# One subtraction per unit instead of two in a two-layer graph network kernel

## The chip, the cores and the metric

The kernel runs on one core of one Trainium2 chip. The metric is the device time of one execution in microseconds; lower is better.

## The reference

Two graph layers follow each other on 4096 nodes with 256 channels. The adjacency matrix `adj` is 4096 x 4096 in float32, 64 MB.

```python
def layer0(x, adj, w):
    A = adj + eye(4096)
    d = rsqrt(sum(A, axis=1))
    return elu(((A * d[:, None] * d[None, :]) @ x) @ w)
def layer1(x, adj, W, b):
    return relu((adj @ x) @ W.T + b)
x = layernorm(x + layer0(x, adj, w))
x = layernorm(x + layer1(x, adj, W, b))
```

## The kernel before

**Units and chunks.** The matrix is cut into chunks of 512 rows by 1024 columns (`raw`, 2 MB, four transfers of 512 KB issued on SP's queue) and each chunk into up to two units of 512 x 512. A unit is the amount that TensorE multiplies at one go. There are 128 units, and the text numbers them 0 to 127 in the order of the list `units`, in which every engine takes them. Units 0 to 28 belong to pass A (the row sums are made, and what of layer 0 can be multiplied already is), 29 to 91 to pass B (the rest of layer 0 and the first part of layer 1), 92 to 127 to pass C (the rest of layer 1). A "row" is a group of 512 nodes; eight of them are finished in B and eight in C. All 84 chunks are read from HBM again in each pass that needs them. `raw` has three buffers in A, and two from the first chunks of B on.

**What a unit goes through.** VectorE (DVE) turns it by a blockwise transposition (`turn`, L479, `turned`). ScalarE (ACT) rounds it to the short float format that TensorE takes (`hi`, L343, `a_hi`), in two halves of 128 x 1024. DVE subtracts, which gives the rest (`lo`, L496, `a_lo`), in two halves too. TensorE (PE) runs 24 matmuls of 128 x 512 on it (`product`, L710 to L712), half 0 first, then half 1: v_hi times a_hi, v_hi times a_lo, v_lo times a_hi. `turned`, `a_hi` and `a_lo` have two buffers each, taken in turns, so that unit u+2 writes where unit u was.

**The waits.** All go by counting semaphores; `halves_of(u, half)` is 2u + half + 1. PE asks for half 0 of `hi` and `lo` before its first twelve matmuls of a unit and for half 1 before the other twelve, and adds one to `s_used` after each half. `hi(u)` asks, half by half, that PE has used that half of unit u-2 and that `lo` of it is done. `turn(u)` asks for both second halves of u-2. An SP load of a chunk into a buffer asks that the last unit of the chunk before it in that buffer has been turned.

**The order on each engine** is written out by the loops over the chunks. On DVE it is turn(u), lo(u-1), turn(u+1), lo(u) and so on, in A as turn, turn, lo, row sums, lo where a chunk has two units. Between them come the steps of rows that are finished, each so many units after the row's last unit: `aggregate` (L545, two instructions, PSUM), `residual` (L556, or L561 and L565 in layer 1), and `v_low` (L525), which waits for `v_hi` from ACT. On ACT it is hi(u), and behind it the steps of a finished row: `elu_parts` (L395 to L401), `moments` (L410, L416), `normalise` (L428) with `v_hi` (L432) or the stores (L435). PE's own steps between units are `project` (L678), `project_x` (L657) and `fold_degrees` (L636).

The functions that the change touches, and what calls them:

Of the kernel before, what the change touches and what calls it, by code (L numbers as in the profile page):

```python
# [33 lines left out]
F32 = mybir.dt.float32  # L34
F32R = mybir.dt.float32r
ALU = mybir.AluOpType
# [4 lines left out]
def gnn_two_layers(nc: bass.Bass, x: bass.AP, adj: bass.AP, w: bass.AP, W: bass.AP, b: bass.AP, out: bass.AP):  # L41
# [96 lines left out]
    def halves_of(u, half):  # L138

        return 2 * u + half + 1  # L140


    HALVES = [(0, slice(0, GT // 2)), (1, slice(GT // 2, GT))]

    with ExitStack() as ctx:  # L145
        def sb(name, shape, dt=F32):
            return ctx.enter_context(nc.sbuf_tensor(name, shape, dt))

        def sem(name):
            return ctx.enter_context(nc.semaphore(name))  # L150
# [5 lines left out]
        turned = [sb(f"turned{i}", [P, GT, GN]) for i in range(2)]  # L156
        a_hi = [sb(f"a_hi{i}", [P, GT, GN], F32R) for i in range(2)]
        a_lo = [sb(f"a_lo{i}", [P, GT, GN], F32R) for i in range(2)]
# [49 lines left out]
        s_hi = sem("hi_halves_ready")  # L208
        s_lo = sem("lo_halves_ready")
        s_used = sem("halves_used")  # L210
# [258 lines left out]
        def _(dve):  # L469
# [19 lines left out]
            def lo(u):  # L489

                dve.wait_ge(s_turn, u + 1)
                for half, part in HALVES:
                    dve.wait_ge(s_hi, halves_of(u, half))
                    if u >= 2:
                        dve.wait_ge(s_used, halves_of(u - 2, half))
                    nc.vector.tensor_tensor(a_lo[u % 2][:, part, :], turned[u % 2][:, part, :],  # L496
                                            a_hi[u % 2][:, part, :].bitcast(F32),
                                            ALU.subtract).then_inc(s_lo, 1)

            def deg_part(n):  # L500
                _, row, panel, _ = chunks[n]
# [66 lines left out]
            def low_and_later(u):  # L568

                if lows_done[0] > u:  # L570
                    return
                lows_done[0] = u + 1
                lo(u)
                for a in ended(u, AGG_AT, rows_done):
                    aggregate(a)
                for a in ended(u, RESIDUAL_AT, rows_done):
                    residual(a)
                for a in ended(u, NORM_AT, rows_done):
                    if accs[a][2] == 0:
                        v_low(GROUPS + order_of[a], accs[a][1])  # L580
# [9 lines left out]
            for n, (name, row, panel, mine) in enumerate(chunks):  # L590
# [18 lines left out]
                if 0 <= last < DIAGONALS and at == 0:  # L609
                    deg_row(last)  # L610
            lo(U - 1)
            for u in range(U - 1, U + NORM_AT + 1):
                for a in ended(u, AGG_AT, rows_done):
# [142 lines left out]
```

## Time and profile before

| what | us |
|---|---|
| median of 3 runs | 953.71 |
| lowest and highest run | 950.77, 953.84 |
| span of the profiled execution, first to last instruction | 945.9 |
| PE busy, share of the span | 798.6, 84% |
| DVE busy | 736.0, 78% |
| ACT busy | 530.9, 56% |
| POOL busy | 101.9, 11% |

The profile is of one execution. It gives its span, and no time of its own beside that; the median of the runs is 7.8 us above the span, which is what lies before the first and behind the last instruction. In the views every row of a timeline begins with start and duration in microseconds from the start of the span; a row marked x2 holds two instructions back to back, and its duration runs from the start of the first to the end of the second. Brackets at its end give the idle time before it and what ended it.

### The profile page before, as it was taken

The page shows a single profiled execution, that of the slowest core. Times are in us where ns is not written, and L with a number is a line of the kernel's source. Part 1 is how long each engine was busy: PE and PEld are TensorE (multiplying, and loading weights), DVE is VectorE, ACT ScalarE, POOL GpSimd, SP SyncE. Part 2 cuts the span into 40 slices and gives each one's busy share as a digit, 9 for nine tenths or more (in the row PEclk, how much of TensorE's full clock was granted, in tenths as well). Part 3 has the DMA queues.
Part 4 walks back from the last instruction along what each step waited for, and adds up shares of the span by engine and source line. Part 5 has one row for each costly group of instructions (what it writes and reads, how often), then busy time and mean ns, then how long its engine had stood idle before and what let it go on. Part 6 is the DMA issues. An engine that isn't in the chain of part 4 may idle for free. (4 is left out here: it accounts for less than half of the span.)

```text
span 945.9 us, 10551 instructions
## 1 busy us (share of the span) xinstructions
PE 798.6 (84%) x3524; PEld 656.8 (69%) x3524; DVE 736.0 (78%) x537; ACT 530.9 (56%) x1192; POOL 101.9 (11%) x108
## 2 busy tenths in 40 slices
PE   0151756569989999999999999999999999999993
PEld 0041635457768888888888888888887778888882
DVE  0454636579979878989898898988987979888861
ACT  2153535367777764475676757667573665455352
POOL 0000000000000000021110211202110231122020
PEclk9995777788999999999999999999999999999997
DMA  9999999999999999998999999999999799998900
GB/s 215 221 219 221 221 220 220 221 225 238 228 230 227 203 206 216 208 219 180 199 209 197 201 207 193 212 191 220 195 211 212 171 211 209 219 219 181 198 23 22
DMA packets 191972, 190.08 MB, mean 201 GB/s; under 512 B 6960, under 2 KB 191920, under 8 KB 191920
## 3 DMA queue, kind: packets, MB, share of 16 engines
q1 hardware_dynamic: 187312, 185.23, 96.2%
q10 hardware_dynamic: 4608, 4.20, 1.5%
q8 instruction: 28, 0.46, 0.2%
q14 instruction: 24, 0.20, 0.1%
HBM read 185.20 MB, written 4.19 MB: 200 GB/s over the span
## 5 line engine op out<-in xcount | busy, mean ns | idle before, releaser
L710 PE MATMUL acc<-a_hi,v_hi 128*128 128x512 f32 x1024 | 411.7, 402 | 35.6 <-DVE a_lo L496 31.4
L343 ACT ACTIVATE a_hi<-turned 128x1024 fp32r<-128x1024 f32 x256 | 265.2, 1058 | 309.5 <-DVE turned L479 151.6
L711 PE MATMUL acc<-a_lo,v_hi 128*128 128x512 f32 x1024 | 406.3, 397 | 0.0
L712 PE MATMUL acc<-a_hi,v_lo 128*128 128x512 f32 x1024 | 406.0, 396 | 0.0
L479 DVE STREAM_TRANSPOSE turned<-raw 128x2048 f32<-128x2048 f32 x128 | 294.1, 2305 | 85.2 <-DMA raw<-in_adj_dram 78.6
L496 DVE TENSOR_TENSOR a_lo<-turned,a_hi 128x1024 fp32r<-128x1024 f32 x256 | 301.4, 1215 | 23.4 <-ACT a_hi L343 15.0
L710 PEld LDWEIGHTS acc<-a_hi,v_hi 128*128 128x128 f32 x1024 | 197.3, 193 | 80.3 <-issue 28.7
L712 PEld LDWEIGHTS acc<-a_hi,v_lo 128*128 128x128 f32 x1024 | 196.9, 192 | 42.3
L711 PEld LDWEIGHTS acc<-a_lo,v_hi 128*128 128x128 f32 x1024 | 197.4, 193 | 40.7
L353 ACT ACTIVATE acc<-raw 128x256 f32<-128x256 f32 x236 | 86.8, 368 | 47.1 <-DMA raw<-in_adj_dram 47.1
L503 DVE TENSOR_REDUCE deg_parts<-raw 128x10 f32<-128x2560 f32 (+4 forms) x32 | 78.1, 2444 | 27.0 <-DMA raw<-in_adj_dram 27.0
L636 PE MATMUL acc<-deg_sums,fold 128*32 128x4 f32 x64 | 2.1, 194 | 52.5 <-DVE deg_sums L512 52.5
L302 POOL TENSOR_TENSOR dinv<-deg,minus_half 128x4 f32<-128x4 f32 x8 | 11.0, 1375 | 329.2 <-DVE deg L520 329.2
L312 POOL TENSOR_TENSOR raw<-raw,x_row 128x1024 f32<-128x1024 f32 x8 | 22.1, 2763 | 223.3 <-ACT raw L399 223.3
L353 ACT ACTIVATION_READ_ACCUMULATOR acc<-raw 128x1 f32 x236 | 44.2, 187 | 0.0
L636 PEld LDWEIGHTS acc<-deg_sums,fold 128*32 128x32 f32 x64 | 1.4, 124 | 55.2 <-DVE deg_sums L512 54.5
L416 ACT ACTIVATE raw<-raw,minus_mean 128x256 f32<-128x256 f32 x64 | 31.8, 498 | 12.7 <-issue 6.4
L428 ACT ACTIVATE normed<-raw,shift,rstd 128x256 f32<-128x256 f32 x64 | 33.2, 590 | 8.1 <-POOL shift L332 8.1
L525 DVE TENSOR_TENSOR v_lo<-normed,v_hi 128x1024 fp32r<-128x1024 f32 x16 | 19.5, 1222 | 22.1 <-ACT v_hi L432 17.5
L410 ACT ACTIVATE raw<-raw 128x256 f32<-128x256 f32 x64 | 25.6, 402 | 19.0 <-DVE raw L565 19.0
L323 POOL TENSOR_SCALAR minus_mean<-sums 128x4 f32<-128x4 f32 x16 | 9.9, 621 | 239.4 <-ACT raw L410 239.4
L657 PE MATMUL proj<-w_sb,x_row 128*128 128x256 f32 x128 | 31.0, 398 | 1.1 <-ACT x_row L372 1.1
(43 smaller groups left out, 347.3 us busy)
## 6 DMA issues: line engine op xcount, KB each, us to landing
raw<-in_adj_dram SPq DMA_DIRECT2D x336, 512.0 KB, 10.4
x_row<-in_x_dram SPq DMA_DIRECT2D x64, 128.0 KB, 9.3
out_dram<-normed ACTq DMA_DIRECT2D x32, 128.0 KB, 2.7
w_sb<-in_L_gnn_w_dram SPq DMA_DIRECT2D x1, 256.0 KB, 12.4
normed<-in_L_gnn_W_dram SPq DMA_DIRECT2D x1, 256.0 KB, 10.7
b_sb<-in_L_gnn_b_dram SPq DMA_DIRECT2D x1, 128.0 KB, 10.1
```

The costliest lines, as they stand in the source:

```text
L343: nc.scalar.activation(a_hi[u % 2][:, part, :], turned[u % 2][:, part, :], ACT.Copy).then_inc(s_hi, 1)
L353: nc.scalar.activation(junk[:, i % JUNK, :], raw[buffer_of[n]][:, k, :], ACT.Copy, accum_out=deg_parts[:, row % 2, panel, k:k + 1]).then_i ...
L410: nc.scalar.activation(neg[:, t, :], res[:, t, :], ACT.Copy, accum_out=sums[:, t:t + 1]).then_inc(s_sums, 1)
L416: nc.scalar.activation(neg[:, t, :], res[:, t, :], ACT.Square, bias=minus_mean[:, t:t + 1], accum_out=squares[:, t:t + 1]).then_inc(s_sq, 1)
L428: nc.scalar.activation(normed[:, t, :], res[:, t, :], ACT.Identity, scale=rstd[:, t:t + 1], bias=shift[:, t:t + 1]).then_inc(s_norm, 1)
L479: ins = nc.vector.transpose(dst, src)
L496: nc.vector.tensor_tensor(a_lo[u % 2][:, part, :], turned[u % 2][:, part, :], a_hi[u % 2][:, part, :].bitcast(F32), ALU.subtract).then_inc ...
L503: nc.vector.tensor_reduce(deg_parts[:, row % 2, panel, mine], raw[buffer_of[n]][:, mine, :], AX_X, ALU.add).then_inc(s_degd, 1)
L657: ins = pe.matmul(proj[:, t, :], flat[:, GN * h + P * t:GN * h + P * (t + 1)], w_sb[:, h, :], start=(h == 0), stop=(h == CH - 1))
L710: pe.matmul(dst, v_hi[:, k, ch], a_hi[u % 2][:, t, :], start=begin, stop=False)
L711: pe.matmul(dst, v_hi[:, k, ch], a_lo[u % 2][:, t, :], start=False, stop=False)
L712: ins = pe.matmul(dst, v_lo[:, k, ch], a_hi[u % 2][:, t, :], start=False, stop=end)
```

## The change

`lo` becomes one subtraction over the whole unit, 128 x 2048. It waits for the second half of `hi(u)` and, from unit 2 on, for the second half of unit u-2 to have been used by PE, and then adds 2 to `s_lo` when it ends. Nothing else is edited: `hi` stays in halves, PE still asks half by half, and what others wait for on `s_lo` has the same numbers.

```diff
             def lo(u):
 
                 dve.wait_ge(s_turn, u + 1)
-                for half, part in HALVES:
-                    dve.wait_ge(s_hi, halves_of(u, half))
-                    if u >= 2:
-                        dve.wait_ge(s_used, halves_of(u - 2, half))
-                    nc.vector.tensor_tensor(a_lo[u % 2][:, part, :], turned[u % 2][:, part, :],
-                                            a_hi[u % 2][:, part, :].bitcast(F32),
-                                            ALU.subtract).then_inc(s_lo, 1)
+                dve.wait_ge(s_hi, halves_of(u, 1))
+                if u >= 2:
+                    dve.wait_ge(s_used, halves_of(u - 2, 1))
+                nc.vector.tensor_tensor(a_lo[u % 2][:], turned[u % 2][:], a_hi[u % 2][:].bitcast(F32),
+                                        ALU.subtract).then_inc(s_lo, 2)
```

## Rows read from the trace of the kernel before

**Rows 1.** Windows: length, busy per engine, granted clock, DMA share, GB/s.

```profile
0.00:280.00 280.00, 152.52 (x630) 122.32 (x631) 162.19 (x106) 136.97 (x437) 11.02 (x24) 0.86 1.12 223
280.00:926.00 646.00, 642.28 (x2880) 531.55 (x2878) 570.06 (x428) 388.04 (x736) 89.20 (x80) 1.00 0.95 197
```

**Rows 2.** DVE groups kept apart by shape: busy us, mean ns, idle before.

```profile
L496 DVE TENSOR_TENSOR a_lo<-turned,a_hi 128x1024 fp32r<-128x1024 f32 x256 | 301.4, 1215 | 23.4 <-ACT a_hi L343 15.0 <-issue 4.1 <-PE acc L712 3.5
L479 DVE STREAM_TRANSPOSE turned<-raw 128x2048 f32<-128x2048 f32 x128 | 294.1, 2305 | 85.2 <-DMA raw<-in_adj_dram 78.6 <-DVE a_lo L496 0.5
...
L486 DVE TENSOR_TENSOR turned<-turned,ident 128x128 f32<-128x128 f32 x32 | 7.2, 287 | 0.3
```

**Rows 3.** Timeline of DVE, 501 to 512 us.

```profile
501.31 1.23 DVE L525 TENSOR_TENSOR v_lo<-normed,v_hi 128x1024 fp32r<-128x1024 f32 x1 [2.17 <-ACT v_hi L432]
502.45 2.31 DVE L479 STREAM_TRANSPOSE turned<-raw 128x2048 f32<-128x2048 f32 x1
504.69 2.31 DVE L496 TENSOR_TENSOR a_lo<-turned,a_hi 128x1024 fp32r<-128x1024 f32 x2
509.34 2.32 DVE L496 TENSOR_TENSOR a_lo<-turned,a_hi 128x1024 fp32r<-128x1024 f32 x2
```

**Rows 4.** Timeline of PE: first matmuls of units 57 and 58.

```profile
506.21 0.39 PE L710 MATMUL acc<-a_hi,v_hi 128*128 128x512 f32 x1
...
511.65 0.39 PE L710 MATMUL acc<-a_hi,v_hi 128*128 128x512 f32 x1
```

**Rows 5.** Timelines of DVE and PE at unit 71.

```profile
583.22 2.32 DVE L496 TENSOR_TENSOR a_lo<-turned,a_hi 128x1024 fp32r<-128x1024 f32 x2
...
584.55 0.47 PE L710 MATMUL acc<-a_hi,v_hi 128*128 128x512 f32 x1 [0.20 <-DVE a_lo L496]
```

**Rows 6.** Timeline of ACT and DVE, from PE's wait to v_lo.

```profile
529.09 1.06 ACT L343 ACTIVATE a_hi<-turned 128x1024 fp32r<-128x1024 f32 x1 [1.61 <-PE acc L712]
...
534.26 2.00 ACT L343 ACTIVATE a_hi<-turned 128x1024 fp32r<-128x1024 f32 x2
...
539.00 1.06 ACT L432 ACTIVATE v_hi<-normed 128x1024 fp32r<-128x1024 f32 x1
...
540.09 1.23 DVE L525 TENSOR_TENSOR v_lo<-normed,v_hi 128x1024 fp32r<-128x1024 f32 x1 [2.16 <-ACT v_hi L432]
```

**Rows 7.** Timelines of DVE and PE at unit 18.

```profile
278.25 2.32 DVE L496 TENSOR_TENSOR a_lo<-turned,a_hi 128x1024 fp32r<-128x1024 f32 x2
...
279.58 0.47 PE L710 MATMUL acc<-a_hi,v_hi 128*128 128x512 f32 x1 [4.07 <-DVE a_lo L496]
```

**Rows 8.** Timelines of DVE and PE at units 43 and 85.

```profile
426.77 2.31 DVE L496 TENSOR_TENSOR a_lo<-turned,a_hi 128x1024 fp32r<-128x1024 f32 x2
...
428.22 0.40 PE L710 MATMUL acc<-a_hi,v_hi 128*128 128x512 f32 x1
...
660.92 2.32 DVE L496 TENSOR_TENSOR a_lo<-turned,a_hi 128x1024 fp32r<-128x1024 f32 x2
...
662.66 0.39 PE L710 MATMUL acc<-a_hi,v_hi 128*128 128x512 f32 x1
```

**Rows 9.** Timelines of DVE, ACT and PE around units 99 and 103.

```profile
742.65 3.73 DVE L496 TENSOR_TENSOR a_lo<-turned,a_hi 128x1024 fp32r<-128x1024 f32 x2
743.83 1.06 ACT L343 ACTIVATE a_hi<-turned 128x1024 fp32r<-128x1024 f32 x1 [1.61 <-PE acc L712]
...
774.67 2.32 DVE L496 TENSOR_TENSOR a_lo<-turned,a_hi 128x1024 fp32r<-128x1024 f32 x2
...
776.00 0.47 PE L710 MATMUL acc<-a_hi,v_hi 128*128 128x512 f32 x1 [1.20 <-DVE a_lo L496]
```

**Rows 10.** Timelines of ACT, DVE and PE at unit 127.

```profile
916.83 2.01 ACT L343 ACTIVATE a_hi<-turned 128x1024 fp32r<-128x1024 f32 x2 [1.94 <-issue]
...
917.98 2.36 DVE L496 TENSOR_TENSOR a_lo<-turned,a_hi 128x1024 fp32r<-128x1024 f32 x2 [4.13 <-issue]
...
920.51 0.39 PE L710 MATMUL acc<-a_hi,v_hi 128*128 128x512 f32 x1
```

## The prediction

> **What bounds the kernel now.** I read the windows first. From 280 to 926 us PE is busy for 642.3 of 646 us at the full granted clock; before 280 us it is busy for 152.5 of 280 us, while the DMA share stands at 1.12 and the adjacency comes in at 223 GB/s [rows 1]. So there are two stages: up to unit 18 the loads set the pace, and from there to the last unit PE does. The reader is to see that DVE, at 570 of 646 us, and DMA, at 0.95, are close behind PE in the second stage, but that neither is what ends last. A microsecond taken from DVE there is worth nothing by itself; a microsecond in which PE waits is lost, unless PE would have waited for something else later.
>
> The groups by shape give the prices on DVE: a subtraction of 1024 columns 1215 ns, of 128 columns 287 ns, a transposition of 2048 columns 2305 ns [rows 2]. The timelines then show how far ahead of PE the low halves are. This is the view that decides. PE starts unit 57 at 506.21 us and unit 58 at 511.65 us, 5.44 us apart [rows 4]. The two subtractions of unit 57 begin at 504.69 us and the pair ends at 507.00 us [rows 3]. PE starts while the second of them is still running: it needs only half 0 then, and asks for half 1 twelve matmuls (2.72 us) later.
>
> **The change part by part.** (1) *The instruction.* The pair takes 2.31 to 2.32 us from its first start to its last end [rows 3]. The two sizes of subtraction give (1215 - 287) / 896 = 1.036 ns a column and a fixed part of 287 - 128 x 1.036 = 154 ns [rows 2]. Two instructions already overlap (2 x 1.215 = 2.43 against 2.31 us), so of the 154 ns about 120 are hidden now. The trace shows no subtraction of 2048 columns. Below, it can cost 2.31 - 0.15 = 2.16 us; above, 2.31 us, which is what the transposition of the same width takes. I take 2.24 us, the middle, so 0.07 us less work on DVE per unit, 128 x 0.07 = 9 us in all. I cost this at nothing, since DVE is not what ends last in either stage.
>
> The Trainium skill (VectorE: DVE Perf Modes, Rules for kernel authors) says to minimise the count of DVE operations and not the semaphores, because the pipe is drained after each one anyway. That speaks for the change; with DVE as the bound the sum would be a gain of 9 us, and by the windows, where PE is the bound, it is none.
>
> (2) *The signal.* PE's wait for half 0 of `lo` now ends when the whole unit is done. Where PE waits for it in the trace, its first matmul starts 0.11 us after the first half ended: at unit 71 the pair starts at 583.22, its first half ends about 1.22 later, at 584.44, and PE starts at 584.55 us [rows 5]. The new start of PE can be no earlier than start of the subtraction + 2.24 + 0.11, that is + 2.35 us. At unit 57 this is 504.69 + 2.35 = 507.04 against 506.21 us: PE waits 0.83 us [rows 3, 4].
>
> I made this sum for all 128 units. In pass B the shortage comes back once per finished row, at the first low halves behind `v_low`. DVE stands 2.2 us there, waiting for `v_hi`, then takes 1.15 us for `v_low` and 2.24 us for the transposition in hand, and only then subtracts [rows 3]. Seven units have it: 0.90 at unit 43, 0.65 at 50, 0.83 at 57, 0.60 at 64, 1.02 at 71, 0.84 at 78, 0.61 at 85; the first and the last are 426.77 + 2.35 - 428.22 and 660.92 + 2.35 - 662.66 [rows 8]. Sum 5.45 us. After each, DVE's lead grows again (a turn and a pair are 4.65 us apart, from 504.69 to 509.34 [rows 3], against PE's 5.44), and the units between are in time once PE is shifted.
>
> Does each stall shift all that follows, or does DVE get back on time? The next `v_low` hangs on PE: `hi` waits for PE at 529.09, `moments` follow it on ACT without a gap to 534.26, then `hi` and `normalise`, `v_hi` ends at 540.06 and `v_low` starts at 540.09 us [rows 6]. Whatever PE loses, this chain passes on to DVE, so the next shortage is as large as before, and the stalls add up.
>
> At unit 18, where PE-bound running begins, the shortage is 278.25 + 2.35 - 279.58 = 1.02 us [rows 7]. PE has no gap after it that it could make this up in. It covers units 29 and 33, which would be short by 0.55 and 0.85 us by themselves, but whose subtractions are paced by loads and so not shifted. Units 2, 4, 7 and 9 are short by 1.02 too; there PE idles later anyway, and I cost them at nothing.
>
> (3) *The wait for both halves of hi.* In pass C `hi` follows the stores on ACT and is itself the late one. At unit 127 the two halves of `hi` run from 916.83 to 918.84, and the subtraction starts at 917.98, after the first [rows 10]. Now it starts at about 918.89 and PE at 918.89 + 2.35 = 921.24 against 920.51 us: 0.73 us. The same pattern at units 114 and 120 gives 0.71 and 0.78. Together 2.2 us. At unit 99 the pair takes 3.73 us because its second half waits for `hi`, whose second half ends at 744.89 [rows 9]; the merged one ends at 744.94 + 2.24 = 747.18 instead of 746.38, so the two turns behind it, the buffer of `raw` and SP's load into it (next in SP's queue) come 0.80 us later, and unit 103's transposition waits for that load. There the shortage itself is 774.67 + 2.35 - 776.00 = 1.02 [rows 9], less 0.07 for the one merged pair ahead of it. Units 92 and 95 are short by 0.91 and 1.02, but PE waits for loads in between, and I count them at nothing. With 0.2 us taken off for the merged pairs ahead of unit 97 this stretch gives 0.80 + 0.95 - 0.2 = 1.5 us.
>
> (4) The wait for `s_used` of half 1 of unit u-2 costs nothing: in B and C PE has begun unit u-1, or `hi` of half 1, which waits for the same, is the later one.
>
> **Sum.** 1.0 + 5.45 + 1.5 + 2.2 = 10.2 us. The span goes from 945.9 to 956.1 us, and the 7.8 us outside it stay: 953.71 + 10.2 = 963.9 us. 0.3% (2.9 us) is about what a measurement of this kernel can tell from no change.
>
> **The rivals.** *The merge pays (faster).* If DVE set the pace, 9 us would be won: 944.7 us. For it: DVE is idle only once per row in B, 2.2 us [rows 3], and once that idle time belongs to the loop the saved time counts. Against it: PE is busy 99.4% of the stage [rows 1], and `v_low` waits for a chain that begins at PE. It decides only if the merged instruction is so short that unit 57's end comes before PE: 506.21 - 0.11 - 504.69 = 1.41 us, under what any row allows. The page named above would have this as the case to expect. Chance 0.04.
>
> *The stalls do not add up.* A stall gives ACT and DVE time, and if `v_low` did not move with PE, every second shortage would be covered by the shift of the first. Then about half is left, 5 us: 958.8 us. For it: units 29 and 33 behave so. Against it: rows 6. Chance 0.16.
>
> *No change.* PE's queue absorbs it, for instance if the 0.23 us between matmuls could shrink after a wait. Nothing in the rows shows PE catching up. 953.7 us, chance 0.06.
>
> *More than the sum.* Shortages that I counted as covered (29 and 33: 1.4 us; 92 and 95: 1.9 us) come on top, and the merged instruction takes 2.31 us (12 stalls x 0.07 = 0.8): 968.0 us. Chance 0.16. A drop of PE's granted clock after a stall would lie there too; against it, the clock is 1.00 over the whole stage from 280 us, which has an idle time of 1.20 us in it already [rows 1, 9].
>
> **The numbers.** The forecast as summed has 0.58. Its own range is 961 to 967 us: 2.16 us instead of 2.24 takes 1.0 off, the stretch of units 92 to 103 may be 0.95 or less, and one covered stall more or less is 1 us. The range for 8 in 10 reaches to the case of half the stalls below and to the case above: 957 to 969 us. Faster 0.04; same, within 0.3%, 0.08 (the case of no change and a little of the half case); slower 0.88.
>
> **What would show it.** Rows of L496 x128 with a mean near 2.3 us (as a record, some 0.03 above the start-to-end price). PE's idle time put down to `a_lo` L496 in the stage from 280 us on grows from about 2 us in three places to about 12 us in some fourteen, each of 0.6 to 1.1 us, one per row of B, right behind `v_low`. DVE's busy time falls by 7 to 11 us. The period of a row in B, 38.8 us now (501.31 to 540.09 [rows 3, 6]), grows by 0.6 to 1.0 us. The granted clock stays 1.00. It would be wrong if the places are fewer (something else on ACT or DVE moved ahead), if the loads in C begin to be the later ones, or if the merged instruction costs more than 2.31 us.

## The result, and the profile after

The changed kernel takes 983.92 us (median of 4 runs, 978.01 to 985.05) against 953.05 us before (4 runs): ratio 1.0331, 95% interval 1.0292 to 1.0369, 31 us slower. The direction was as forecast; the size is three times the 10.2 us of the sum, and outside the range.

The head of the page after, with the groups that answer to [rows 2] (the subtraction is now L495, PE's matmuls L708 to L710):

```profile
span 981.8 us, 10423 instructions
## 1 busy us (share of the span) xinstructions
PE 806.4 (82%) x3524; PEld 658.7 (67%) x3524; DVE 739.1 (75%) x409; ACT 529.3 (54%) x1192; POOL 99.7 (10%) x108
...
L708 PE MATMUL acc<-a_hi,v_hi 128*128 128x512 f32 x1024 | 415.2, 405 | 64.3 <-DVE a_lo L495 60.3
L343 ACT ACTIVATE a_hi<-turned 128x1024 fp32r<-128x1024 f32 x256 | 265.0, 1057 | 338.8 <-PE acc L710 189.3
...
L495 DVE TENSOR_TENSOR a_lo<-turned,a_hi 128x2048 fp32r<-128x2048 f32 x128 | 300.4, 2347 | 65.7 <-ACT a_hi L343 64.6
...
L323 POOL TENSOR_SCALAR minus_mean<-sums 128x4 f32<-128x4 f32 x16 | 21.4, 1338 | 264.9 <-ACT raw L410 264.9
```

Half of the subtractions are gone, and DVE is busy for 739 us where it was 736. The prediction had it fall by 7 to 11 us; six subtractions of pass C that take 2.7 to 4.1 us bring about 9 us back. The idle time of DVE before the subtraction, waiting for `a_hi`, rose from 15.0 [rows 2] to 64.6 us. One row was not looked at in the prediction: GpSimd's `minus_mean`, 128 x 4 elements, now takes 1338 ns on average, while `var_eps`, of the same size and engine, takes 0.19 us.

The tile's own view gives the durations of the subtraction (min/median/max, in ns) and who waits for it, from 280 us on:

```profile
L495 DVE TENSOR_TENSOR a_lo<-turned,a_hi x110: 2244/2291/4134, 282.9 to 952.5; 128x2048 fp32r<-128x2048 f32 x110
...
  PE acc L708: 28.7, 18
```

The shortest is 2.244 us, the price that the prediction took; the median is 2.29 us, and four take 4.13 us. PE waits for the low halves 18 times. One of these waits is unit 18's, 7.4 us against 4.07 us before [rows 7]. The other 17 come to 21.3 us, up to 2.8 us each in pass C, where the prediction had about 12 us in some fourteen places.

**A first check of the yardstick.** The profiled execution of the changed kernel took 983.62 us with a span of 981.8, so 1.8 us lie around a span, and not the 7.8 us that stand ahead of the prediction. The first profile of the kernel before was of a quick execution. The two traces therefore differ by 35.9 us, of which some 4 us are not the change's. What is shifted where is read from the start of PE's first matmul of each unit. Against the first trace of before, the changed kernel's is later by 8.0 us at unit 29, 19.1 at unit 92, 19.2 at unit 107, and 35.9 at unit 127. Pass B loses 11 us and pass C 17 us, nearly all of it behind unit 107, in four steps at units 108, 113, 119 and 126.

**One step of pass C, unit 108.** Timelines of DVE, POOL and ACT (ACT's accumulator reads left out):

```profile
817.97 2.25 DVE L495 TENSOR_TENSOR a_lo<-turned,a_hi 128x2048 fp32r<-128x2048 f32 x1
820.36 2.31 DVE L479 STREAM_TRANSPOSE turned<-raw 128x2048 f32<-128x2048 f32 x1
824.58 4.13 DVE L495 TENSOR_TENSOR a_lo<-turned,a_hi 128x2048 fp32r<-128x2048 f32 x1 [1.91 <-ACT a_hi L343]
...
817.99 2.32 POOL L323 TENSOR_SCALAR minus_mean<-sums 128x4 f32<-128x4 f32 x1 [19.25 <-ACT raw L410]
...
824.02 0.20 POOL L332 TENSOR_TENSOR shift<-minus_mean,rstd 128x4 f32<-128x4 f32 x1
824.17 2.39 POOL L318 TENSOR_TENSOR x_row<-v_hi,v_lo 128x1024 f32<-128x1024 f32 x1
...
820.40 0.51 ACT L416 ACTIVATE raw<-raw,minus_mean 128x256 f32<-128x256 f32 x1 [2.49 <-issue]
...
822.39 1.99 ACT L343 ACTIVATE a_hi<-turned 128x1024 fp32r<-128x1024 f32 x2
```

The same place in the trace before (POOL, DVE, ACT), with one `minus_mean` of pass B ahead of it:

```profile
531.83 0.36 POOL L323 TENSOR_SCALAR minus_mean<-sums 128x4 f32<-128x4 f32 x1 [7.58 <-ACT raw L410]
...
798.81 1.15 POOL L323 TENSOR_SCALAR minus_mean<-sums 128x4 f32<-128x4 f32 x1 [17.94 <-ACT raw L410]
...
803.67 0.78 POOL L332 TENSOR_TENSOR shift<-minus_mean,rstd 128x4 f32<-128x4 f32 x1
804.41 3.40 POOL L318 TENSOR_TENSOR x_row<-v_hi,v_lo 128x1024 f32<-128x1024 f32 x1
...
803.17 2.36 DVE L496 TENSOR_TENSOR a_lo<-turned,a_hi 128x1024 fp32r<-128x1024 f32 x2 [0.49 <-ACT a_hi L343]
...
800.05 0.51 ACT L416 ACTIVATE raw<-raw,minus_mean 128x256 f32<-128x256 f32 x1 [1.32 <-issue]
```

Three things come together. First, `minus_mean` begins 0.02 us after a subtraction and ends 0.09 us after it (820.31 against 820.22): it waits the subtraction out. That took 1.15 us when the subtraction had 1024 columns and takes 2.32 us now; where DVE is in a transposition, as at 754.78 us of the same trace, `minus_mean` takes 0.23 us. ACT, which needs it for the squares, stands 2.49 instead of 1.32 us, with `hi` of unit 108 queued behind. Second, the subtraction of unit 108 has to wait for both halves of this late `hi` (to 824.38). Third, in that time GpSimd's addition of 128 x 1024 gets to start at 824.17, and now it is DVE that waits: the addition ends at 826.56, and the subtraction that "began" at 824.58 ends 2.15 us after that. Before, GpSimd's `shift` waited out the first half's subtraction (0.78 us instead of 0.20), so the addition behind it came after the start of the second half's, and took 3.40 instead of 2.39 us. PE had lead enough that this cost nothing.

PE stands 2.72 us for it, and its matmuls then start 0.42 us apart instead of 0.23:

```profile
828.86 0.47 PE L708 MATMUL acc<-a_hi,v_hi 128*128 128x512 f32 x1 [2.72 <-DVE a_lo L495]
...
829.63 0.62 PE L708 MATMUL acc<-a_hi,v_hi 128*128 128x512 f32 x1
830.05 0.63 PE L709 MATMUL acc<-a_lo,v_hi 128*128 128x512 f32 x1
```

Unit 108's matmuls take 6.9 us from first to last start, where 5.2 is usual: the granted clock is 0.50 (1.2 GHz, the lower of its two levels) from 829.6 to 833.0 us, and 1.00 (2.4 GHz) before and behind. That costs 1.7 us more. Together 4.6 us for one row.

**The same wait in pass B**, at the `moments` ahead of unit 56 (DVE, ACT), and PE at units 56 and 57:

```profile
503.01 2.28 DVE L495 TENSOR_TENSOR a_lo<-turned,a_hi 128x2048 fp32r<-128x2048 f32 x1
505.40 2.31 DVE L479 STREAM_TRANSPOSE turned<-raw 128x2048 f32<-128x2048 f32 x1
509.64 2.29 DVE L495 TENSOR_TENSOR a_lo<-turned,a_hi 128x2048 fp32r<-128x2048 f32 x1 [1.93 <-ACT a_hi L343]
512.53 1.23 DVE L523 TENSOR_TENSOR v_lo<-normed,v_hi 128x1024 fp32r<-128x1024 f32 x1 [0.60 <-ACT v_hi L432]
...
505.47 0.51 ACT L416 ACTIVATE raw<-raw,minus_mean 128x256 f32<-128x256 f32 x1 [2.46 <-issue]
...
512.08 0.47 PE L708 MATMUL acc<-a_hi,v_hi 128*128 128x512 f32 x1 [0.89 <-DVE a_lo L495]
...
518.30 0.47 PE L708 MATMUL acc<-a_hi,v_hi 128*128 128x512 f32 x1 [0.49 <-DVE a_lo L495]
```

The stall at unit 57 is the predicted one. The one at unit 56, ahead of `v_low`, was not in the sum.

### The profile page after: what moved, and what is told of

Read it like the earlier page. It is cut to its first block and busy times, and to the rows that moved or that the text cites. A ratio compares the mean times of both kernels' runs of the same rounds, so it can differ in the third digit from the quotient of the medians.

```text
span 981.8 us, 10423 instructions
## 1 busy us (share of the span) xinstructions
PE 806.4 (82%) x3524; PEld 658.7 (67%) x3524; DVE 739.1 (75%) x409; ACT 529.3 (54%) x1192; POOL 99.7 (10%) x108
## 5 line engine op out<-in xcount | busy, mean ns | idle before, releaser
L708 PE MATMUL acc<-a_hi,v_hi 128*128 128x512 f32 x1024 | 415.2, 405 | 64.3 <-DVE a_lo L495 60.3
L710 PE MATMUL acc<-a_hi,v_lo 128*128 128x512 f32 x1024 | 407.4, 398 | 0.0
L495 DVE TENSOR_TENSOR a_lo<-turned,a_hi 128x2048 fp32r<-128x2048 f32 x128 | 300.4, 2347 | 65.7 <-ACT a_hi L343 64.6
L708 PEld LDWEIGHTS acc<-a_hi,v_hi 128*128 128x128 f32 x1024 | 198.3, 194 | 114.8 <-issue 69.0
L710 PEld LDWEIGHTS acc<-a_hi,v_lo 128*128 128x128 f32 x1024 | 197.9, 193 | 42.8
L323 POOL TENSOR_SCALAR minus_mean<-sums 128x4 f32<-128x4 f32 x16 | 21.4, 1338 | 264.9 <-ACT raw L410 264.9
L312 POOL TENSOR_TENSOR raw<-raw,x_row 128x1024 f32<-128x1024 f32 x8 | 19.3, 2417 | 230.6 <-ACT raw L399 230.6
L676 PE MATMUL proj<-wt_sb,raw 128*128 128x256 f32 x128 | 29.1, 380 | 1.5 <-DVE raw L545 1.4
```

Source lines behind the costliest of these rows:

```text
L495: nc.vector.tensor_tensor(a_lo[u % 2][:], turned[u % 2][:], a_hi[u % 2][:].bitcast(F32), ALU.subtract).then_inc(s_lo, 2)
L676: ins = pe.matmul(proj[:, t, :], nodes, wt_sb[:, h, :], start=(h == 0), stop=(h == CH - 1))
L708: pe.matmul(dst, v_hi[:, k, ch], a_hi[u % 2][:, t, :], start=begin, stop=False)
L710: ins = pe.matmul(dst, v_lo[:, k, ch], a_hi[u % 2][:, t, :], start=False, stop=end)
```

## The experiments

Times are against runs of the kernel before on the same chip (951.07 to 952.84 us medians); "+x us" is the ratio's excess times that, and for the changed kernel it is +31.5 us (27.8 to 35.2). The table "Start of unit" at the end of the section collects all traces.

**The kernel before once more, and the merge in one pass at a time.** The edit of the three against the changed kernel, here for pass A:

```diff
+                if units[u][0] == "A":
+                    dve.wait_ge(s_hi, halves_of(u, 1))
...
+                                            ALU.subtract).then_inc(s_lo, 2)
+                else:
+                    for half, part in HALVES:
...
```

> The kernel before, profiled once more as a control. The first profile had a span of 945.9 us, while its timed runs (950.8 to 953.8 us) would have spans of about 949 to 952 us if 1.8 us lie around a span, as in the runs of the changed kernel. If the 8.0 us that unit 29 starts later in the changed kernel's trace are partly the luck of one execution's loads, this trace starts unit 29 at 353 to 356 us instead of 350.9 and its span is 949 to 952 us. If they all belong to the change, unit 29 starts at 350.9 again, within 0.5 us.

> One subtraction only for the units of pass A (0 to 28), two elsewhere. The sum on record gives +1.0 us (unit 18 alone); the rival reading of the two traces, by which the whole later start of unit 29 is the change's, gives +8 us. A shift of 1 to 3.5 us would say that a stall of PE or a delay on ScalarE near the end of A counts beside unit 18.

> One subtraction only for the units of pass B (29 to 91). The sum on record gives +5.5 us, one stall of PE per row. The trace of the changed kernel shows 11.1 us between units 29 and 92, with a second stall of 0.6 to 0.9 us per row at the unit ahead of the predicted one: +9 to +12 us if that belongs to the change in B itself.

> One subtraction only for the units of pass C (92 to 127). The sum on record gives +3.7 us. The trace of the changed kernel shows 16.8 us from unit 92 to unit 127, 4.1 to 4.6 us of it per row at units 108, 113 and 119 and 2.9 at 126: +15 to +18 us if nothing from A and B is needed for it, with subtractions of about 4.1 us at four or five places.

The control took 947.41 us with a span of 945.6: 1.8 us around the span again, but also a quick execution, so its unit 29 starts where the first one's does (0.6 us sooner), not at the 353 to 356 us that I expected of a typical one; it doesn't tell how late a typical one would be. Pass A alone: ratio 1.0032 (1.0011 to 1.0052), +3.0 us. Pass B alone: 1.0109 (1.0069 to 1.0150), +10.4 us. Pass C alone: 1.0173 (1.0137 to 1.0208), +16.5 us. Pass A lies between the 1 us of the sum and the 8 us of the rival reading, B and C where the trace of the changed kernel had put them. The three add up to 29.9 of 31.5 us, so within the intervals nothing depends on two passes being merged at once. The sum on record had 1.0, 5.45 and 3.7. C is where most of the miss lies.

**The parts of the edit, one at a time.** `one_signal` keeps two subtractions and their own waits and signals after the second; `late_start` keeps both signals and puts the waits of the merged kernel in front; `late_one_signal` does both, and so has everything of the change but the long instruction.

```diff
-                    nc.vector.tensor_tensor(a_lo[u % 2][:, part, :], turned[u % 2][:, part, :],
+                    ins = nc.vector.tensor_tensor(a_lo[u % 2][:, part, :], turned[u % 2][:, part, :],
                                             a_hi[u % 2][:, part, :].bitcast(F32),
-                                            ALU.subtract).then_inc(s_lo, 1)
+                                            ALU.subtract)
+                ins.then_inc(s_lo, 2)
```

and for the start:

```diff
+                dve.wait_ge(s_hi, halves_of(u, 1))
+                if u >= 2:
+                    dve.wait_ge(s_used, halves_of(u - 2, 1))
                 for half, part in HALVES:
-                    dve.wait_ge(s_hi, halves_of(u, half))
-                    if u >= 2:
-                        dve.wait_ge(s_used, halves_of(u - 2, half))
```

> Two subtractions with their own waits as before, but both are signalled together when the second ends. This is the signal part alone. The sum on record, without its late starts: 1.0 + 5.5 + 1.0 = 7 to 8 us slower. The rival, by which the late start and GpSimd's traffic with VectorE make most of the 31 us, agrees on this run (6 to 10 us) and says that subtractions stay under 2.6 us and units 108, 113, 119 and 126 lose under 1 us each. If the run is 20 us or more slower, the signal alone is the cause.

> Two subtractions of 1024 columns with a signal each as before, but both wait for the second halves of hi and of s_used up front. This is the start part alone. By the sum on record it costs only where hi is itself late (units 114, 120, 127, 99), and since half 0 is signalled 1.1 us sooner than in the merged kernel, less than 1.5 us. If a late start lets GpSimd's 128 x 1024 addition go first and VectorE wait for it, units 108, 113, 119 and 126 show a first subtraction of about 3 us and the run is 3 to 8 us slower.

> Two subtractions of 1024 columns, but with the waits of the merged kernel in front and its one signal behind: everything of the change except the long instruction. If only waits and signals matter, it is as slow as the changed kernel, 30 to 32 us over the kernel before. If the length of the instruction matters, because GpSimd's minus_mean (L323) has to wait until the subtraction in hand is over (at most 1.15 us here, 2.3 us in the changed kernel), the stalls of units 42, 56, 70 and 84 are gone (3.5 us), those of 108, 113, 119 and 126 fall from 2.9 to 1.9 us and the drops of the clock go (5 us): 18 to 24 us over the kernel before.

`one_signal`: 962.92 us, ratio 1.0115 (1.0085 to 1.0144), +11 us, a little above both expectations. Between units 33 and 91 its trace loses 7.5 us, 6.8 of it at the seven predicted units, 0.8 to 1.2 us each, and from unit 102 on next to nothing. `late_start`: 959.41 us, 1.0084 (1.0054 to 1.0115), +8 us, more than the sum allowed and at the top of what the rival had. Its trace has the addition of GpSimd in front of DVE's subtractions (DVE, then POOL):

```profile
807.73 4.33 DVE L496 TENSOR_TENSOR a_lo<-turned,a_hi 128x1024 fp32r<-128x1024 f32 x2 [0.66 <-ACT a_hi L343]
...
807.44 2.41 POOL L318 TENSOR_TENSOR x_row<-v_hi,v_lo 128x1024 f32<-128x1024 f32 x1
```

The pair takes 4.33 us, where it took 2.36 before, and each of units 108, 113, 119 and 126 loses 0.8 us. `late_one_signal`: 971.89 us, 1.0219 (1.0194 to 1.0244), +20.8 us. So 31.5 - 20.8, about 11 us (6 to 15 by the two intervals), hang on nothing but the length of the instruction. In its trace the four steps are 1.9 us each, without a drop of the clock there, and `minus_mean` gets in between the two subtractions:

```profile
814.22 1.21 POOL L323 TENSOR_SCALAR minus_mean<-sums 128x4 f32<-128x4 f32 x1 [19.11 <-ACT raw L410]
```

The stalls of units 42, 56 and 84 are gone, as expected; unit 70 still loses 0.7 us.

**GpSimd's addition cut short, in both kernels.**

```diff
-                    nc.gpsimd.tensor_tensor(x_row[:], v_hi[:, tiles(row), :].bitcast(F32), v_lo[:, tiles(row), :].bitcast(F32),
+                    nc.gpsimd.tensor_tensor(x_row[:, :, 0:4], v_hi[:, tiles(row), 0:4].bitcast(F32), v_lo[:, tiles(row), 0:4].bitcast(F32),
                                             ALU.add).then_inc(s_resx, 1)
```

> The changed kernel, in which GpSimd's addition of v_hi and v_lo in pass C (L318) is done for 4 of 256 channels only, so that the residual of layer 1 is left incomplete. If VectorE's subtraction and GpSimd's addition exclude each other, the subtractions of 4.1 us fall to about 2.3, and at each of units 108, 113, 119 and 126 the stall of PE falls from 2.8 to about 0.9 us, with the drop of the clock gone: 10 to 14 us faster than the changed kernel, so 970 to 974 us. If the two have nothing to do with each other: 984 us, unchanged.

> The same cut of GpSimd's addition in the kernel before. There the pair of subtractions starts before the addition, and PE has 2.4 us of lead at these units: no change, within 1 us of 953, by both theories. If this run is 5 us or more faster, the cut takes away work that was on the path anyway, and the run with the changed kernel tells less.

In the changed kernel: 972.44 us, ratio to before 1.0213 (1.0186 to 1.0239), so +20 instead of +31.5 us. In the kernel before: 950.92 us, 0.9980 (0.9958 to 1.0003), no change. Both are as expected. The subtraction of unit 108 in the changed kernel with the short addition, and that addition (DVE, POOL):

```profile
822.15 2.29 DVE L495 TENSOR_TENSOR a_lo<-turned,a_hi 128x2048 fp32r<-128x2048 f32 x1 [1.91 <-ACT a_hi L343]
...
821.74 0.22 POOL L318 TENSOR_TENSOR x_row<-v_hi,v_lo 128x16 f32<-128x16 f32 x1
```

4.13 us has become 2.29 us. The wait for `a_hi` in front (1.91 us) stays, and so does `minus_mean` at 2.32 us. The four steps are 1.1 us each, and no unit from 103 on is slow.

**minus_mean on ScalarE instead of GpSimd.**

The edit on GpSimd, and then on ScalarE in `moments`, behind the wait for the sums:

```diff
-                pool.wait_ge(s_sums, GT * (i + 1))
-                if i:
-                    pool.wait_ge(s_sq, GT * i)
-                nc.gpsimd.tensor_scalar(minus_mean[:], sums[:], -1.0 / C, None, ALU.mult).then_inc(s_mean, 1)
```

```diff
+                if i:
+                    act.wait_ge(s_rstd, 3 * i)
+                    act.wait_ge(s_sq, GT * i)
+                nc.scalar.activation(minus_mean[:], sums[:], ACT.Copy, scale=-1.0 / C).then_inc(s_mean, 1)
```

> The changed kernel with minus_mean (128 x 4) made on ScalarE instead of GpSimd, so that it no longer waits for VectorE's subtraction. If that wait is what turns 1.1 us of stall into 2.9 at units 108, 113, 119 and 126 and makes the stalls of 42, 56, 70 and 84: 12 to 16 us faster than the changed kernel, 968 to 972 us, and no drop of the clock in pass C. If it is not: within 2 us of 984 us.

> The changed kernel with both: minus_mean on ScalarE, and GpSimd's addition in pass C for 4 of 256 channels only (the residual of layer 1 is left incomplete). What is left of the change should be what the prediction had: the signal, and late halves of hi. 8 to 12 us over the kernel before, 961 to 965 us, with stalls of PE at units 43, 50, 57, 64, 71, 78, 85 of 0.5 to 1.0 us. Over 968 us would say that a third cause is missing.

> The kernel before with minus_mean on ScalarE: a control for the two above, and a try at a better kernel. PE is busy 99.4% of passes B and C there, so the shorter chain should gain nothing: within 1.5 us of 953 us. If it is faster by 3 us or more, GpSimd's wait for VectorE cost the kernel before something already.

In the changed kernel: 962.46 us, 1.0115 (1.0089 to 1.0141). Of the 31.5 us, 20.6 are gone, more than I expected. With the short addition as well: 957.81 us, 1.0071 (1.0052 to 1.0090), +6.7 us, a little under the expected 8 to 12; of the seven expected stalls in pass B its trace has only unit 78's, 0.55 us. In the kernel before: 951.73 us, 1.0011 (0.9999 to 1.0022), no change. So these two 128 x 4 and 128 x 1024 operations of GpSimd, each taken away by itself, gain the old kernel nothing, and in the changed one they cost 25 us together.

Moving `minus_mean` also saves a handover between two engines. That is worth little: between the last of the sums and the first of the squares ACT stands 0.40 us with `minus_mean` on a GpSimd that nobody holds up, 0.27 us with it on ACT, and up to 2.49 us with it behind the long subtraction (the changed kernel in pass C, then `mean_act_after`, ACT):

```profile
792.55 0.51 ACT L416 ACTIVATE raw<-raw,minus_mean 128x256 f32<-128x256 f32 x1 [0.40 <-ACT raw L410]
...
807.14 0.20 ACT L411 ACTIVATE minus_mean<-sums 128x4 f32<-128x4 f32 x1
807.37 0.51 ACT L416 ACTIVATE raw<-raw,minus_mean 128x256 f32<-128x256 f32 x1
```

In `mean_act_after` the addition is still ahead of DVE (DVE, POOL, unit 108):

```profile
811.79 3.89 DVE L495 TENSOR_TENSOR a_lo<-turned,a_hi 128x2048 fp32r<-128x2048 f32 x1
...
811.13 2.40 POOL L318 TENSOR_TENSOR x_row<-v_hi,v_lo 128x1024 f32<-128x1024 f32 x1
```

but the subtraction comes with more lead, and PE loses 0.7 us there instead of 2.9, with no drop of the clock.

No variant beats the kernel before by more than its interval; `small_add_before` leaves work out and does not either.

**Start of unit** (first matmul, us later than in the first trace of the kernel before; each from one execution):

| kernel | unit 29 | unit 92 | unit 107 | unit 127 |
|---|---|---|---|---|
| before_again | -0.6 | 0.4 | -0.3 | -0.3 |
| changed | 8.0 | 19.1 | 19.2 | 35.9 |
| merge_A_only | 9.2 | 9.4 | 8.0 | 8.0 |
| merge_B_only | 0.4 | 10.8 | 10.4 | 10.7 |
| merge_C_only | 3.1 | 4.3 | 4.0 | 17.8 |
| one_signal | 6.8 | 16.1 | 13.9 | 14.3 |
| late_start | 2.2 | 2.8 | 3.6 | 7.1 |
| late_one_signal | 6.0 | 14.5 | 15.4 | 23.5 |
| small_add_after | 5.1 | 16.1 | 16.8 | 22.9 |
| small_add_before | 0.8 | 0.8 | -0.7 | -0.5 |
| mean_act_after | 5.1 | 7.8 | 8.4 | 11.6 |
| mean_act_small_add_after | 7.1 | 9.6 | 10.0 | 10.2 |
| mean_act_before | 1.9 | 1.6 | 1.4 | 1.4 |

The start of unit 127 less that of unit 107 is the four steps of pass C: 16.7 us in the changed kernel, 13.8 in `merge_C_only`, 0.4 in `one_signal`, 3.5 in `late_start`, 8.0 in `late_one_signal`, 6.1 in `small_add_after`, 3.2 in `mean_act_after` and 0.1 with both of its edits.

## Why the prediction was wrong, by its own steps

In short: GpSimd stands in none of the prediction's terms. Its `minus_mean` and its addition, which wait for DVE's subtraction or hold it up, carry 25 of the 31.5 us. Without them 6.7 us are left, beside 10.2 us forecast, and even those lie partly in other places than the sum had them.

**What bounds the kernel: right.** DVE's time bought nothing and nearly all of PE's new waits were paid.

**(1) The instruction: its price right, its cost at nothing wrong.** The merged subtraction takes 2.25 us behind another instruction and 2.29 us behind an idle time, against 2.24 forecast and 2.31 to 2.36 for most pairs. But "I cost this at nothing, since DVE is not what ends last" looked only at DVE's own time. The long instruction keeps GpSimd out for twice as long, and that is worth 11 us by itself (`late_one_signal` against the changed kernel). This is the step that failed, together with the cost of nothing for units 108, 113, 119 and 126 under (3). The rows were there: the old trace has `minus_mean` at 0.23 us, 0.36 us and 1.15 us in different places. The Trainium skill (SBUF — State Buffer, Who interferes with whom) says that a VectorE instruction with two inputs in SBUF and a GpSimd instruction that reads SBUF exclude each other for the whole of the one that comes first. By that rule the subtraction is such an instruction, and the trace agrees in both directions: GpSimd 2.32 us for 128 x 4 elements, DVE 4.13 instead of 2.25. The prediction weighed the advice for fewer instructions that it names from the Trainium skill, and not this rule.

**(2) The signal: the places and the sum near in pass B, incomplete.** `merge_B_only` loses 0.77, 0.54, 0.77, 0.53, 0.42, 1.44 and 0.78 us at units 43, 50, 57, 64, 71, 78 and 85, together 5.25 against 5.45 us forecast. That the sum fits so well is partly luck: unit 71 is 0.6 us under its forecast and unit 78 is 0.6 us over. They add up and do not cover each other, as argued; the rival by which they would not is refuted. What was missing is a second stall at units 42, 56, 70 and 84 (3.2 us) and 0.55 us at unit 92. Units 29 and 33 lose 1.25 us in `merge_B_only` and nothing in the changed kernel, covered as the prediction said. The sentence that failed is "the units between are in time": the subtraction ahead of `v_low` waits for both halves of a `hi` that is queued behind `moments`, and `moments` behind `minus_mean`. With `minus_mean` on ScalarE the whole of B from unit 29 to 91 costs 0.9 us, the seven predicted stalls included. By the prediction's prices PE has to be 1.15 + 2.24 + 2.35 = 5.74 us behind the start of `v_low`, or it stands. In the old trace it was 4.7 to 5.1 us behind at these seven units; with `minus_mean` on ScalarE it is 6.1 us behind at five of them and 5.8 at units 71 and 78. So the lead of DVE in B was set by GpSimd's wait too, and not by PE alone.

**Pass A: term 1.0 us, measured 3.0 (1.0 to 5.0).** 1.5 us is seen at unit 28 in all seven traces with a late start in A, and not in `one_signal`: PE waits there for the row sums of the last row, 1.94 us in the changed kernel and 0.40 us before.

```profile
349.90 0.25 PE L634 MATMUL acc<-deg_sums,fold 128*32 128x4 f32 x8 [1.94 <-DVE deg_sums L510]
```

In four of the seven (`merge_A_only`, `late_one_signal` and both with `minus_mean` on ScalarE) the granted clock falls to 0.50 for 3.4 us behind this wait, which costs another 1.6 us. The rest stays open: the seven traces with the common signal in A reach unit 29 by 5.1 to 9.2 us late, the others by -0.6 to 3.1, but loads pace this pass and single executions differ by 3 us without any change.

**(3) Both halves of hi: right in kind, less than a quarter of the size.** I had 2.2 us at units 114, 120 and 127 and 1.5 around 99 to 103. At 114, 120 and 127 about 0.5 us each was there (`small_add_after`). But 13.8 us were lost behind unit 107 in `merge_C_only`, nearly all at 108, 113, 119 and 126, 2.9 us each, which the sum has at nothing: in the old trace the second half of `hi` of unit 108 ended at 804.03 and PE began the unit at 806.75 us, so that 804.03 + 0.05 + 2.35 left 0.3 us. Counted from the start of the old subtraction, the lead is 806.75 - 803.17 - 2.35 = 1.2 us, and three delays hit there at once: 1.2 us by `minus_mean`, 0.9 by the second half of `hi`, 1.9 by the addition; 4.0 less 1.2 is 2.8 us. The runs take it apart: the late start alone 0.8 us a row, with the common signal 1.9, with the long instruction 2.9, in the changed kernel with the drop of the clock 4.6; without the addition 1.1, without GpSimd's `minus_mean` 0.7, without both nothing. The group 92 to 103, 1.5 us forecast, came out at 0.7 us from unit 91 to 107 in `merge_C_only` and at 2.0 in the changed kernel. It is a balance: units 92 and 102 start later, and the waits that PE had before units 95 and 97 shrink. No run takes it apart.

**The clock.** A fall was named among the reasons for "more than the sum" and then argued away with an idle time of 1.20 us and a clock of 1.00 over the stage. The 1.00 is a rounded mean: in the old trace the granted clock is 0.50 from 280.3 to 283.7 us, behind the idle time of 4.07 us before unit 18. After idle times of 2.7 to 2.8 us it fell at units 108, 113 and 119 of the changed kernel, which cost 1.5 to 1.7 us each, and at unit 102 after 1.92 us; at unit 126 it did not fall after 2.76 us. In `late_one_signal` it did not fall after 2.50 us before unit 102 nor after the four idle times of 1.7 us, but it did at unit 28 after 1.86 us. In `merge_C_only` it fell at one of the four steps. The length of the idle time alone does not say when; that stays open.

**The 7.8 us around the span** are 1.8 us; this touches the yardstick, not the difference.

## What to carry to other kernels

Before making an instruction of one engine longer, look for every other engine's short instructions that end together with it: a 128 x 4 operation that takes 1.15 us in one place and 0.36 in another is waiting for something that has no semaphore, and here it waited out the longer one, 2.32 us. A merged instruction starts with the last of its inputs and signals with the last of its outputs; where a consumer runs half by half with less lead than half the instruction, both ends are paid. A start that slips can also let another engine go first. Then the parts of the edit can cost more together than their sum: in the last four rows the late start alone was 3.5 us, the common signal alone 0.4, and both 8.0, though over the whole run 8 and 11 against 20.8 us are the same within the intervals. And a small step moved off the shared path (here `minus_mean`) may be worth nothing in a kernel with lead and 20 us in the same kernel without it.

## What the runs showed of the hardware

The order in which VectorE's two-input subtraction and GpSimd's operation start decides which of them pays: GpSimd's 128 x 1024 addition takes 3.40 us behind a subtraction and 2.39 ahead of it, and the subtraction 2.25 or 4.13 us. Two subtractions of 1024 columns back to back let a GpSimd operation in between them: `minus_mean` then takes 1.2 and not 2.3 us. DVE's transposition, which has one input, held neither up here: beside it, in the changed kernel, `minus_mean` takes 0.23 us and the addition 2.40 us.
